# The next image's transposes two tiles sooner, its statistics between the maxima, its group sums in the local banks, and its normalisation ahead of the attention output's eviction

## The reference

```python
x = x + L0(_gn(x), w_qkv, w_proj, b_proj)   # 8 heads of 32, inside windows of 32 positions
x = x + L1(_gn(x), Wq, Wk, Wv, gamma)       # one head, all 1024 positions: energy = k q^T

def _gn(v, G=32, eps=1e-05):                # statistics over an image and 8 channels
    g = v.reshape(B_, H_, W_, G, C_ // G)
    m = jnp.mean(g, axis=(1, 2, 4), keepdims=True)
    s = jnp.var(g, axis=(1, 2, 4), keepdims=True)
    return ((g - m) / jnp.sqrt(s + eps)).reshape(v.shape)
```

## Time and profile before

| | |
|---|---|
| median of 3 runs | 707.22 us |
| the profiled execution, whole | 708.19 us |
| its span, first to last instruction | 706.1 us |
| PE busy | 600.7 us (85%) |
| DVE busy | 493.9 us (70%) |
| ACT busy | 321.7 us (46%) |
| POOL busy | 152.0 us (22%) |
| mean granted TensorE clock | 0.944 of full speed |

### The profile page before, as it was taken

The page is one execution under the profiler, slowest core; times in us unless marked ns, Lnnn a source line. Parts: engine busy times, 40 slices in busy tenths (PEclk is TensorE's granted clock), DMA queues, the critical chain, the costliest instruction groups (busy, mean ns, idle before and its releaser), DMA issues. The chain is left out here.

```text
span 706.1 us, 14862 instructions
## 1 busy us (share of the span) xinstructions
PE 600.7 (85%) x5859; PEld 433.6 (61%) x5859; DVE 493.9 (70%) x829; ACT 321.7 (46%) x422; POOL 152.0 (22%) x130
## 2 busy tenths in 40 slices
PE   2475794799998999899998999899989989649987
PEld 2255472547785677657774778567765767336756
DVE  4445267667976888577976797597967796775654
ACT  2423443476228741675228632774157611750261
POOL 5502232213114202303213311411230321000000
PEclk9996896789999999999999999999999999878999
DMA  4042313231241225031323223122504103201101
GB/s 156 0 121 61 90 32 94 50 82 38 84 105 51 61 54 145 33 88 31 104 82 82 51 82 104 48 56 48 145 26 105 31 24 106 76 0 38 43 4 60
DMA packets 40306, 47.51 MB, mean 67 GB/s; under 512 B 6848, under 2 KB 32320, under 8 KB 40256
## 3 DMA queue, kind: packets, MB, share of 16 engines
q1 hardware_dynamic: 36960, 43.47, 23.5%
q10 hardware_dynamic: 3296, 3.34, 1.4%
HBM read 10.09 MB, written 8.39 MB: 26 GB/s over the span
## 5 line engine op out<-in xcount | busy, mean ns | idle before, releaser
L250 PE MATMUL pb<-v_h,e_h 128*128 128x257 f16 x464 | 127.6, 275 | 1.7 <-DVE y L929 1.6
L252 PE MATMUL pb<-v_h,e_l 128*128 128x257 f16 x464 | 126.5, 273 | 0.0
L251 PE MATMUL pb<-v_l,e_h 128*128 128x257 f16 x464 | 126.1, 272 | 0.0
L904 DVE TENSOR_REDUCE max_neg<-pb 128x1 f32<-128x1024 f32 x64 | 77.5, 1210 | 42.6 <-PE pb L536 42.2
L919 DVE TENSOR_TENSOR e_l<-e,e_h 128x1024 f16<-128x1024 f32 x64 | 77.8, 1223 | 18.9 <-ACT e L744 17.3
L744 ACT ACTIVATE e<-pb,f_energy 128x1024 f32<-128x1024 f32 x64 | 71.3, 1114 | 23.1 <-PE pb L554 23.1
L554 PE MATMUL pb<-k_stack,q_stack 98*128 98x512 f16 x128 | 39.3, 389 | 29.8 <-ACT k_stack L735 19.9
L718 ACT ACTIVATE before_turn<-pa 128x1024 f16<-128x1024 f32 x16 | 15.5, 1021 | 106.5 <-PE pa L484 106.5
L1058 POOL TENSOR_TENSOR xb<-xin,bias 128x2048 f32<-128x2048 f32 x8 | 36.7, 4588 | 125.5 <-DVE x L884 125.5
L250 PE MATMUL pa<-a_nh,wqkv_h 128*128 128x512 f16 x128 | 52.1, 407 | 11.6 <-POOL a_nl L1051 11.6
L1063 POOL TENSOR_TENSOR before_turn<-before_turn,a_rinv 128x1024 f32<-128x1024 f32 x16 | 30.6, 1914 | 140.4 <-DVE a_rinv L865 140.4
(11 more groups left out here) (135 smaller groups left out, 1365.6 us busy)
## 6 DMA issues: line engine op xcount, KB each, us to landing
xin<-in_x SPq DMA_DIRECT2D x16, 512.0 KB, 4.5
diag<-qkT SPq DMA_DIRECT2D x64, 128.0 KB, 2.3
diag<-turned SPq DMA_DIRECT2D x64, 128.0 KB, 2.4
turned<-before_turn SPq DMA_DIRECT2D x128, 64.0 KB, 2.0
out<-y SPq DMA_DIRECT2D x24, 256.0 KB, 2.1
out<-y ACTq DMA_DIRECT2D x8, 256.0 KB, 2.1
q_stack<-qk_hl SPq DMA_DIRECT2D x8, 128.0 KB, 2.3
k_stack<-qk_hl SPq DMA_DIRECT2D x8, 128.0 KB, 2.4
```

What stands on the lines that cost most here:

```text
L250: nc.tensor.matmul(out_ap, lh, rh, start=start, stop=False)
L251: nc.tensor.matmul(out_ap, lh, rl, start=False, stop=False)
L252: return nc.tensor.matmul(out_ap, ll, rh, start=False, stop=stop)
L904: nc.vector.tensor_reduce(max_neg[:, it:it + 1], pb[:, 0:2, :].rearrange("p a n -> p (a n)"), X, ALU.max, negate=True).then_inc(b_max, 1)
```

## The change

Five things, in the first half of a step, unless said otherwise.

1. PE: the transposes of image i+2 stand behind the first energy tile (`it` 1), and no longer in output 3.
2. The group mean and variance of block a are written to banks 1 and 3 of pa, where the transposes have been, and no longer to pb. The mean's matmul comes ahead of `a_output` 0 and the variance's behind it. `a_output` 1 writes these two banks and so waits for DVE's step on the variance (`an_ve`). The wait for it in `b_project_v` is gone.
3. DVE: the statistics are in two parts, behind maximum 2 and behind result 3; group mean and `group_scale` are earlier. Row sum 1 stands ahead of maximum 1, result 2 ahead of the first 32 x 32 transpose, the second 32 x 32 transpose behind the statistics.
4. ACT: `normalise` stands ahead of `a_out_high`.
5. The same in the written-out steps, as far as their flags hold.

SP's order is unchanged, and so is POOL's.

```diff
-        bufs = {"a": dict(..., ps=pa, col=384, mean=3, var=2, ...),
+        bufs = {"a": dict(..., ps=pa, gps=pa, col=384, mean=1, var=3, ...),
...
@@ a_output
                         pe.wait_ge(n_["a"]["xt"], nth(b, 4, 8))
                         pe.nop(nofuse=True)
+                elif b_next:
+
+                    pe.wait_ge(n_["a"]["ve"], nth(b, 1, 2))
+                    pe.nop(nofuse=True)
@@ b_project_v
-                    if f and j == 0:
-
-                        pe.wait_ge(n_["a"]["ve"], nth(b, 1, 3))
-
@@ PE, first
-                    if f and it == 3: transposes("a", i + 2, range(4))
                     if b and it == 2: b_energy(i, 1, m)
                     if o and not last_image(i - 1): b_output(i - 1, it, b, range(4, 8))
                     if b and it >= 1: b_energy(i, (0, 2, 3)[it - 1], m)
+                    if f and it == 1: transposes("a", i + 2, range(4))
...
                     if m and it == 5: a_output(i + 1, f, 0)
+                    if f and it == 5: group_var("a", i + 2)
                     if m and it == 6: a_output(i + 1, f, 1)
...
-                    if f and it == 5: group_mean("a", i + 2)
-                    if f and it == 6: group_var("a", i + 2)
+                    if f and it == 4: group_mean("a", i + 2)
@@ ACT, first
                 if f: copy_T("a", i + 2, range(4))
+                if f: normalise("a", i + 2)
                 if m: a_out_high(i + 1)
-                if f: normalise("a", i + 2)
```

## The result

| | before | after |
|---|---|---|
| median of 8 runs each | 706.76 us (703.02 to 708.43) | 714.30 us (711.29 to 715.88) |
| the profiled execution | 708.19 us | 711.29 us |
| its span | 706.1 us | 709.3 us |
| PE busy | 600.7 us | 601.1 us |
| mean granted TensorE clock | 0.944 | 0.949 |

The changed kernel is slower: ratio 1.0105, 95% interval 1.0084 to 1.0127. Of before, the profile caught an execution near its slowest, of after its fastest. So the two traces are 3.1 us apart where the medians are 7.5 apart. The traces can explain the 3.1. The other 4.4 no trace shows: the mean granted clock of the changed kernel's eight executions lies between 0.931 (in the slowest, 715.88 us) and 0.950 (711.73 us), so more lost clock is the likely place, but it is not shown.

A forecast was written before the change was run, and what follows sets the result against it. PE was taken to set the pace. On the profiled 708.2 us: loop +1.0, clock +1.6, step -1 +5.2, step 0 -1.5, step 6 +0.8, in all +7.1, so 715.3, stated as 715 us; range 706 to 722.

The forecast's parts named there:

- The sum: Whole kernel: all terms together +7.1 us on the profiled 708.2 us, giving 715.3.
- The load: Transposes behind energy 0: PE waits 2.4 us, then 0.5 more, for the image's load; 2.9 us of new idle.
- The rival in which the image is in time: Transposes: the load lands by 342.4, transposed energy 2.0 us sooner a step, 695 us; chance 0.10.
- The mean: PE ahead of `a_output` 0: the mean's matmul waits 1.1 us for DVE's aggregate.
- The loop step: Steps 1 to 5: 3.2 us stall gone, 3.5 us of others ahead; +0.2 us a step, 1.0 in all.
- The clock in the loop: Steps 1 to 5: old stall's loss goes (-5.0), four drops of 1.65 us come (+6.6); net +1.6 us.
- The rival without falls: Loop steps: the new waits have work between them and leave the clock alone; 708 us, chance 0.18.
- Step -1: Written-out step: eviction behind normalisation delays PE's image 1 projection to 78.05 and `a_projection` to 89.9; +5.2 us.
- Step 0: Written-out step: transposed energy 0.3 us sooner, its 3.98 us stall becomes 1.6, half the clock loss regained; -1.5 us.
- Step 6: Written-out step: no transposes to hide row sum 1 and result 2 ahead of maxima 1 and 2; +0.8 us.
- Row and rule: DVE beside POOL: subtractions hold result 5 up to 0.9 us, hidden, and result 6 by 0.1; counted as nothing.
- The output chain: Rival: POOL's copies hold result 6's product up to 1.2 us; about 0.9 us in six steps, 720.5 us; chance 0.12.

The follow-up runs named there:

- Run 1: The changed kernel with SP issuing the load of image i+3 ahead of the four stacking DMAs, not behind them: 698.05 us, ratio 0.9876 to before.
- run 9: The kernel before with only the transposes moved behind energy 0, all other orders as before: 733.80 us, ratio 1.0383.
- run 4: The changed kernel with the load ahead of the stacks, ACT's eviction first in step -1, and the mean's matmul behind output 5's first half: 688.98 us.
- run 6: The changed kernel with ACT's old order, eviction ahead of normalisation, in all steps: 722.17 us, ratio 1.0223 to before.
- run 10: The changed kernel with the transposes back in output 3 and ACT's eviction ahead of normalisation everywhere: 707.37 us, ratio 1.0021 to before.
- run 8: The changed kernel with the transposes back at their old place in output 3, all else as changed: 700.14 us, ratio 0.9911 to before.
- run 2: The changed kernel with the transposes one place later on PE, behind energy 1 instead of energy 0: 697.15 us, ratio 0.9859 to before.
- run 3: The changed kernel with ACT's old order, eviction ahead of normalisation, in step -1 alone: 713.20 us, ratio 1.0081 to before.

## Why the prediction was right, step by step

It said 715, with slower and the same near even; 714.30 was measured. The mechanism held: the wait for the load, the lost clock and step -1's eviction. The sum, made from one execution, is 4 us too high between the two traces and right between the medians, which is partly luck.

*The load.* 2.4 + 0.5 us were forecast, 2.27 + 0.18 measured in step 3, 1.70 to 2.35 elsewhere. Run 1 shows it to be the cause and run 9 its price without the other items. The rival in which the image is in time (695 us) is close to what run 1 built: 698.05.

*The mean.* 1.1 us forecast, 0.91 to 0.98 measured in steps 1 to 5; run 4 removes it.

*The loop step.* +0.2 forecast, +0.3 measured in step 4, the one that kept its clock. ACT began to normalise 21.5 us behind energy 0 there (444.01), 21.4 forecast. The 3.2 us stall went, as forecast.

*The clock in the loop.* Four falls of five, forecast and found. They cost less than 1.65 each: with step 4's 76.31 us as the base, steps 1, 2, 3 and 5 lost 0.75, 1.5, 1.7 and 1.3. In part that is the base, since step 4 had the longest wait for the load (2.35 us, step 1 2.09), and in step 1 the low stretch began 0.5 us before the wait was over; the rest was not traced. The term was +1.6 and measured +0.1 (5.2 us lost against 5.1 before). The rival without falls (708, in which 0.5 us has no source) is refuted by the clock rows.

*Step -1.* +5.2 forecast; energy 0 came 4.7 later, although the prologue before it was 0.5 us shorter (10.68 us to PE's first instruction instead of 11.19). 5.2 is right, and its two dates, 78.05 and 89.9, were 77.50 and 89.35.

*Step 0.* The term that was mis-sized most: -1.5 forecast, -3.0 measured. The transposed energy comes 0.6 us sooner (29.34 behind energy 0 for 29.95), its stall of 3.98 us is gone altogether, where one of 1.6 was forecast to be left, and from there the step is 2.4 us shorter (42.64 for 45.07), which is all of the clock loss and not half.

*Step 6.* +0.8 forecast, +0.15 measured (72.27 us against 72.12). The waits for maxima 1 and 2 are there, 1.97 us for the first:

```profile
582.32 0.59 PE L536 MATMUL pb<-q_stack,k_stack 96*128 96x512 f16 x2 [1.97 <-DVE max_neg L904]
```

but 0.82 us of wait for a result of DVE and 0.40 us for the regrouped image have gone. That leaves 0.7 us, of which 0.15 was measured; what gave the other half microsecond back was not traced.

*The sum.* The measured terms (+1.6, +5.2, -3.0, +0.15) make +3.9, against +7.1 forecast, and with 0.5 us less in the prologue and 0.2 at the end they are the 3.2 us between the traces. The medians are 7.5 us apart: the changed kernel's other seven executions took 0.4 to 4.6 us more than the profiled one, and where they lost it no trace shows. That these 4.4 us and the 4.0 by which the sum is too high nearly cancel is luck.

*Row and rule.* DVE's and POOL's timelines of step 3:

```profile
369.51 0.97 DVE L927 TENSOR_TENSOR y_fac<-y_inv,f_out 128x1 f32<-128x1 f32 x1
...
374.58 0.16 DVE L927 TENSOR_TENSOR y_fac<-y_inv,f_out 128x1 f32<-128x1 f32 x1
```

```profile
369.29 1.17 POOL L1054 TENSOR_TENSOR a_nl<-a_xT,a_nh 128x512 f16<-128x512 f32 x1 [1.70 <-ACT a_xT L692]
...
373.53 1.16 POOL L1054 TENSOR_TENSOR a_nl<-a_xT,a_nh 128x512 f16<-128x512 f32 x1 [0.25 <-ACT a_xT L692]
374.63 1.17 POOL L1073 COPY y<-x 128x512 f32<-128x512 f32 x2
```

Result 5's product was held until POOL's subtraction ended (370.48 and 370.46), 0.8 us (up to 0.9 was forecast), and nobody waited for it. Result 6's took its plain 0.16 us, from 374.58 to 374.74, around the recorded end of a subtraction (374.69) and the recorded start of the copies (374.63). The output chain did not become the bound in the changed kernel; in runs 6 and 10, where the subtractions come later, it did hold PE for 1.1 us a step. The Trainium skill (SBUF — State Buffer, "SBUF: two separate sides") has the instruction that starts first take the shared pair for its whole length; the trace agrees with that for result 5 (and run 6's for result 7), and for result 6 the times are too close to tell. The rival had counted on the copies holding this product, and they did not.

## What to carry to other kernels

Before an instruction is moved forward, look up when its input lands and what that transfer stands behind on its queue: here the same move cost 14 us with one load issued behind four stacks, and nothing with it ahead of them (run 1 against run 8; the load ahead with the transposes back was not built). A reordering pays by the stall that it removes only if the idle time is not put elsewhere; count where each wait goes, and look at the written-out steps before and behind the loop, where the order that is right for the loop can be wrong. Where a step can lose its clock, count a wait with the fall it may bring: in these steps 0.75 to 1.7 us on top of a wait of 2.1 to 2.3. And where an engine's work is moved later, look at what it then runs beside: POOL's subtractions held DVE's small products in both orders, with no wait of PE's in the one and 1.1 us a step in the other.

## What was not expected of the hardware

The granted clock fell to 0.50 in four steps of five of the changed kernel, on waits for the load of 2.07 to 2.27 us a moment after one of 0.5 to 0.8; the step that was spared had the longest of these waits, 2.35 us. With 0.8, 0.4 and 0.2 us (run 2) no step lost it. The ten executions of run 3 lie between 707.2 and 717.6 us, with mean clocks of 0.926 to 0.945; which steps fall in each was recorded for one only. And in three kernels (runs 3, 4 and 10) the clock stayed at 0.50 for the whole of step -1's middle, in which the second half of the attention output took 3.64 us instead of 1.95 (the first half took 3.3 to 3.6 us in every trace); run 10's row:

```profile
67.28 3.64 PE L488 MATMUL pa<-diag,v_tok 128*32 128x128 f32 x64 [0.46 <-DVE ave L829]
```
